# Rows in by sixteen indexed gathers and out by sixteen indexed scatters on GpSimd, in place of eight plain transfers on SyncE

## The chip, the core and the metric

The kernel runs on one core of a Trainium2 chip. The metric is the device time of one execution in microseconds (us). The program is written out by hand: every engine has its own list of instructions, and they meet only at semaphores. The engines are TensorE (PE, its weight loads PEld), VectorE (DVE), ScalarE (ACT), GpSimd (POOL) and SyncE (SP, whose transfer instructions are shown as SPq).

## The reference, cut to what matters

A network of four layers over 8 sequences of 256 tokens with 128 features, 2048 rows of 128 f32 values (512 bytes a row):

```
x = L0_attn_x                      # (8, 256, 128)
... layer norm, mixture-of-experts FFN, 4 linear-attention blocks,
... a second such FFN, a capacity-routed FFN, 16-head causal attention, the routed FFN again
return x                           # (8, 256, 128)
```

Which rows are read and written does not depend on data: row r of the input is token r, and row r of the result is token r. The arithmetic between is the same in both kernels.

## The kernel before

The activations are kept transposed in SBUF, features on the partitions and the 2048 tokens along the free dimension, in four blocks of 512 tokens (`NTB` = 4 blocks of `TB` = 512, `TPB` = 4 tiles of 128 rows to a block, `TILES` = 16 in all).

**Load.** SyncE issues four transfers first of all (L424), each of a block of 512 rows (256 KB) into `x_tok`, with a semaphore `x_loaded[t]` for each block. Behind them stand its loads of the first expert's weights, some twenty small rows of parameters, and the eight large loads of `w0_raw` for the other experts (L443 to L448).

**Constants.** GpSimd meanwhile writes the constants. First comes the identity matrix `ident` (a memset, then an affine select, L2106 and L2108, which announces `ident_ready`), then the mean weights and the epsilons (`const_ready` 1), then selection masks and iotas (`const_ready` 2). Its next work is in the first FFN: one subtraction for each product tile (`fl`, L2138).

**Start of the compute.** TensorE waits for `ident_ready`, then for each block waits for `x_loaded[t]` and transposes its four tiles (L1140). ScalarE copies each block to `xr` (L1530), and TensorE, ScalarE and VectorE do the first layer norm. VectorE begins with `centre` (L2082), made from `ident`, and then splits the first expert's weights (L1550).

**End.** TensorE transposes the four blocks back (L1159), ScalarE copies each to `z` and announces `out_copied` (L1541), and SyncE stores each block with one transfer (L518) and waits for all (`out_stored`). GpSimd has nothing in its list behind the last weight split of the last FFN (L2155).

Of the kernel before, what the change touches and what calls it, by code (L numbers as in the profile page):

```python
# [9 lines left out]
I32 = mybir.dt.int32  # L10
# [4 lines left out]
P = 128  # L15
SEQS, SEQ = 8, 256
TOK = SEQS * SEQ
TB = 512
NTB = TOK // TB
TILES = TOK // P  # L20
TPB = TB // P
# [111 lines left out]
def f32(ap):  # L133
    return ap.bitcast(F32)


def macaron(nc, a, const, out):
# [3 lines left out]
    with es:  # L141
        def sem(name):
            return es.enter_context(nc.semaphore(name))
# [20 lines left out]
        sb = Region(top)  # L164
        xr = sb("xr", [P, TOK])
        z = sb("z", [P, TOK])
# [10 lines left out]
        iota_p = sb("iota_p", [P, 2])  # L177
        iota_t = sb("iota_t", [P, SEQ])
        eps = sb("eps", [P, 3])
        ln_v = sb("ln_v", [P, NTB, TPB])  # L180
        ln_r = sb("ln_r", [P, NTB, TPB])
        ln_t = sb("ln_t", [P, NTB, TPB])
# [29 lines left out]
        x_tok = fd("x_tok", [P, TILES, P])  # L212
# [146 lines left out]
        x_loaded = [sem(f"x_loaded{t}") for t in range(NTB)]  # L359
# [55 lines left out]
        outT_ready, out_copied, out_stored = sem("outT_ready"), sem("out_copied"), sem("out_stored")  # L415
# [3 lines left out]

        @block.sync  # L420
        def _(sp):
            xf = a["L0_attn_x"].rearrange("s t d -> (s t) d")
            for t in range(NTB):
                sp.dma_start(x_tok[:, t * TPB:(t + 1) * TPB, :],  # L424
                             xf[t * TB:(t + 1) * TB, :].rearrange("(q p) d -> p q d", p=P)).then_inc(x_loaded[t], 16)
            sp.dma_start(w0_raw[:, 0, 0:H0], a["L0_ffn_sw1"][0]).then_inc(w0_loaded[0], 16)
            sp.dma_start(w0_raw[:, 0, H0:2 * H0], a["L0_ffn_sw3"][0]).then_inc(w0_loaded[0], 16)
            sp.dma_start(w0_raw[:, 0, 2 * H0:W0].rearrange("p (t d) -> p t d", t=HT0),
# [83 lines left out]
            for e in range(EXP // 2, EXP):  # L512
                load_up(1, e)

            of = out.rearrange("s t d -> (s t) d")
            for t in range(NTB):
                sp.wait_ge(out_copied, t + 1)
                sp.dma_start(of[t * TB:(t + 1) * TB, :].rearrange("(q p) d -> p q d", p=P),  # L518
                             z[:, t * TB:(t + 1) * TB].rearrange("p (q d) -> p q d", q=TPB)).then_inc(out_stored, 16)
            sp.wait_ge(out_stored, 16 * NTB)  # L520

        W0_LOADS, W0_EARLY, W0_LATE = (3, 4, 4), (4, 5, 6, 7), (6, 8, 10, 12)

# [1 line left out]
        def _(pe):  # L525
# [609 lines left out]

            pe.wait_ge(ident_ready, 1)
            for t in range(NTB):
                pe.wait_ge(x_loaded[t], 16)
                for q in range(TPB):
                    ins = pe.transpose(ps[:, XT_BANKS[t], q * P:(q + 1) * P], x_tok[:, t * TPB + q, :], ident[:])  # L1140
                ins.then_inc(xT_ready, 1)
# [961 lines left out]
        def _(pool):  # L2103
            own = Steps(pool, pool_step)

            own.did(pool.memset(ident[:], 0.0))  # L2106
            own.wait()
            pool.affine_select(out=ident[:], in_=ident[:], pattern=[[-1, P]], compare_op=ALU.not_equal,  # L2108
# [35 lines left out]
            def ffn1(call):  # L2144

                def turned(tb):
                    pool.wait_ge(xtf_done, NTB * call + tb + 1)
                    pool.wait_ge(xth_done, NTB * call + tb + 1)
                    w = slice(tb * TPB, (tb + 1) * TPB)
                    pool.tensor_tensor(xt_lo[:, w, :], xtf[:, tb % 2, :].rearrange("p (q d) -> p q d", d=P), f32(xt_hi[:, w, :]),  # L2150
                                       ALU.subtract).then_inc(xt_done, 1)

                def split_low(e):
                    pool.wait_ge(w1_hi_done, call * EXP + e + 1)
                    pool.tensor_tensor(w1_lo[:, e, :], w1_raw[:, e % (EXP // 2), :], f32(w1_hi[:, e, :]), ALU.subtract).then_inc(w1_lo_done, 1)  # L2155

                if call == 1:
                    for e in range(EXP // 2):
                        split_low(e)
                    pool.wait_ge(proj_ready, NTB)  # L2160
                for tb in range(SPB):
                    turned(tb)
                if call == 0:
                    for e in range(EXP // 2):
                        split_low(e)
                for tb in range(SPB, NTB):
                    turned(tb)
                for e in range(EXP // 2, EXP):
                    split_low(e)
# [16 lines left out]
            def attn1():  # L2186

                for s in range(SEQS):
                    for n in range(3):
                        pool.wait_ge(exp_done, 3 * s + n + 1)  # L2190
                        e = ex[:, s % 2, n, :, :].rearrange("p g (h t) -> p g h t", t=P if n == 2 else SEQ)[:, :, :, 0:P]
                        pool.affine_select(out=e, in_=e, pattern=[[0, 4], [0, 4 if n == 2 else 2], [1, P]],  # L2192
                                           compare_op=ALU.is_ge, fill=0.0, base=0, channel_multiplier=-1).then_inc(causal_done, 1)
# [11 lines left out]
            attn1_masks()  # L2205
            attn1()
            ffn1(1)


def _const():  # L2210
# [49 lines left out]
```

## Time and profile before

| | |
|---|---|
| median of 2 runs | 1089.91 us (1087.03 and 1092.79) |
| span of the profiled execution | 1083.3 us |
| between that span and the runs | 3.7 to 9.5 us, 6.6 us to the median |
| busy: PE, DVE, ACT, POOL | 87%, 65%, 57%, 30% of the span |
| on the chain that ended last: PE, DVE, ACT, POOL, DMA | 65%, 18%, 10%, 2%, 0% |

The span runs from the first to the last instruction of the profiled execution. No separate device time of that execution is given, so its own time is read as the median of the runs. The busy shares are averages over the whole span; the chain of waits says for each moment which engine's work the rest waited for. Instructions that issue transfers are not counted as busy.

### The profile page before, as it was taken

Reading aid. Unit: us, or ns where it says so; the run is one execution under the profiler, and the core shown is the slowest. Engines: PE = TensorE matmul, PEld = TensorE weight load, DVE = VectorE, ACT = ScalarE, POOL = GpSimd, SP = SyncE. Lnnn points to the kernel's source line nnn. Section 1 sums busy time; section 2 is a strip of 40 time slices with the busy share of each in tenths; the row PEclk is TensorE's granted clock in tenths of the full one; section 3 lists DMA queues with packets and bytes.
Section 4 is the critical chain, followed back from the end, with each engine's and each line's share of the span. In section 5 each row is a group of like instructions: output and inputs, shape, how many; then the busy total and the mean of one; then the engine's idle time right before and its main releaser. Section 6 shows DMA issues by size and latency. Waiting matters only on the chain.

```text
span 1083.3 us, 13006 instructions
## 1 busy us (share of the span) xinstructions
PE 945.4 (87%) x4507; PEld 638.9 (59%) x4507; DVE 703.1 (65%) x1413; ACT 615.0 (57%) x995; POOL 326.4 (30%) x241
## 2 busy tenths in 40 slices
PE   6899999579999999879999995899777787788997
PEld 4678886223333333337888875688554555465896
DVE  3978887467778777746788887733276556347532
ACT  6455555268888888763555554544644545535443
POOL 1597776000000000002777774200101211313100
PEclk8999999789999999997999998899978879757999
DMA  5225110000000000003321211100000000001001
GB/s 171 42 79 159 65 64 24 0 1 0 1 1 1 0 1 0 1 0 117 81 68 59 68 41 49 49 2 1 1 2 2 4 3 2 4 1 39 2 1 39
DMA packets 30743, 33.64 MB, mean 31 GB/s; under 512 B 2062, under 2 KB 19798, under 8 KB 30678
## 3 DMA queue, kind: packets, MB, share of 16 engines
q1 hardware_dynamic: 30678, 32.81, 10.3%
q8 instruction: 36, 0.59, 0.2%
q14 instruction: 29, 0.24, 0.1%
HBM read 31.36 MB, written 1.18 MB: 30 GB/s over the span
## 4 chain that ended last, share of the span: by engine, by line
PE 65%; DVE 18%; ACT 10%; issue 4%; POOL 2%; DMA 0%; SPq 0%; ACTq 0%; DVEq 0%; POOLq 0%
PE ps L128 10%; PE ps L129 10%; PE ps L130 10%; PE ps L745 5%; PE ps L857 5%; PE ps L878 3%; PE ps L739 2%; PE ps L943 2%; PE ps L723 2%; ACT L1362 2%; ACT ex L1468 2%; DVE smax L2017 2%; POOL fl L2138 2%; PE ps L828 1%; PE ps L731 1%
## 5 line engine op out<-in xcount | busy, mean ns | idle before, releaser
L2138 POOL TENSOR_TENSOR fl<-fp,fh 128x512 fp32r<-128x512 f32 x144 | 223.3, 1566 | 126.8 <-ACT fh L1268 126.6
L1259 ACT ACTIVATE fs<-ps 128x512 f32<-128x512 f32 x144 | 86.4, 600 | 114.5 <-PE ps L130 114.4
L1726 DVE TENSOR_TENSOR fp<-fp,cwb 128x512 f32<-128x512 f32 x128 | 140.8, 1100 | 14.0 <-DVE fp L1719 0.9
L1719 DVE TENSOR_TENSOR fp<-fs,ps 128x512 f32<-128x512 f32 x144 | 98.1, 682 | 40.7 <-ACT fs L1259 40.2
L128 PE MATMUL ps<-z_hi,w_hi 128*128 128x512 f32 x288 | 116.8, 405 | 3.3 <-DVE fp L1719 3.2
L129 PE MATMUL ps<-z_lo,w_hi 128*128 128x512 f32 x288 | 116.0, 403 | 0.0
L130 PE MATMUL ps<-z_hi,w_lo 128*128 128x512 f32 x288 | 115.9, 402 | 0.0
L1268 ACT CAST fh<-fp 128x512 fp32r<-128x512 f32 x144 | 88.8, 617 | 36.8 <-DVE fp L1726 32.7
L2199 POOL TENSOR_TENSOR ln_sq<-ln_rs 128x512 f32<-128x512 f32 x20 | 21.2, 1058 | 272.3 <-ACT ln_rs L1325 272.3
L2192 POOL TENSOR_SCALAR_AFFINE_SELECT ex<-ex 128x1024 f32<-128x1024 f32 (+1 forms) x24 | 33.5, 1406 | 155.2 <-ACT ex L1468 155.2
L2017 DVE TENSOR_REDUCE smax<-ps 128x8 f32<-128x2048 f32 (+1 forms) x24 | 54.9, 2291 | 38.4 <-PE ps L957 33.3
L1409 ACT ACTIVATE hid<-ps 128x512 f32<-128x512 f32 x64 | 38.4, 601 | 50.3 <-PE ps L130 49.5
L128 PEld LDWEIGHTS ps<-z_hi,w_hi 128*128 128x128 f32 x288 | 55.5, 193 | 18.9 <-DVE fp L1719 5.6
L857 PE MATMUL ps<-hid,w 128*128 128x256 f32 x256 | 66.0, 383 | 0.0
L739 PE MATMUL ps<-z,wb 128*128 128x512 f32 x128 | 62.6, 616 | 2.7 <-DVE qq L1823 2.7
L130 PEld LDWEIGHTS ps<-z_hi,w_lo 128*128 128x128 f32 x288 | 55.6, 193 | 12.9
L129 PEld LDWEIGHTS ps<-z_lo,w_hi 128*128 128x128 f32 x288 | 55.4, 192 | 12.6 <-issue 0.2
L128 PE MATMUL ps<-fh,w_hi 128*128 128x512 f32 x144 | 57.5, 399 | 3.8 <-POOL fl L2138 3.8
L731 PE MATMUL ps<-z,wb 128*128 128x512 f32 x96 | 51.1, 675 | 10.7 <-DVE z L1798 10.7
L745 PE MATMUL ps<-hid,wb 128*128 128x512 f32 x128 | 60.1, 593 | 0.0
L727 PE MATMUL ps<-ln_sq,mean_w 128*128 128x512 f32 x72 | 39.3, 628 | 20.1 <-ACT ln_sq L1318 20.1
L129 PE MATMUL ps<-fl,w_hi 128*128 128x512 f32 x144 | 56.8, 395 | 0.0
(264 smaller groups left out, 1997.9 us busy)
## 6 DMA issues: line engine op xcount, KB each, us to landing
cwb<-cw_spread SPq DMA_DIRECT2D x64, 256.0 KB, 3.2
w_raw<-in_L_ffn_w_dram SPq DMA_DIRECT2D x20, 256.0 KB, 2.8
w_raw<-in_L_ffn_w_dram SPq DMA_DIRECT2D x4, 512.0 KB, 5.7
w<-in_L_ffn_w_dram SPq DMA_DIRECT2D x8, 256.0 KB, 4.5
x_tok<-in_L_attn_x_dram SPq DMA_DIRECT2D x4, 256.0 KB, 3.6
wb<-in_L_attn_W_dram SPq DMA_DIRECT2D x1, 1024.0 KB, 6.9
wb<-in_L_attn_W_dram SPq DMA_DIRECT2D x4, 256.0 KB, 4.0
out_dram<-z SPq DMA_DIRECT2D x4, 256.0 KB, 3.0
```

Of the source, the lines that this page charges most:

```text
L128: pe.matmul(out, w_hi, x_hi, start=start, stop=False)
L129: pe.matmul(out, w_hi, x_lo, start=False, stop=False)
L130: return pe.matmul(out, w_lo, x_hi, start=False, stop=stop)
L739: pe.matmul(ps[:, bank, :], wb[:, b, (4 + k) * P:(5 + k) * P], blk(z, t), start=True, stop=True).then_inc(a0_matmul[t], 1)
L745: pe.matmul(ps[:, A0_WO, :], wb[:, b, w], hid[:, k, :], start=(k == 0), stop=(k == FT - 1)).then_inc(a0_matmul[t], 1)
L857: ins = pe.matmul(ps[:, OUT1[n % 2], 0:SEQ], w2[:, e, ft * P:(ft + 1) * P], hid[:, g % RING1, f * SEQ:(f + 1) * SEQ], start=(ft == 0), sto ...
L1259: act.activation(fs[:, n % 2, :], ps[:, n % 2, :], ACT.Silu).then_inc(silu_done, 1)
L1268: act.copy(fh[:, n % RING0, :], fp[:, n % RING0, :]).then_inc(fhi_done, 1)
L1719: dve.tensor_tensor(f, fs[:, n % 2, :], ps[:, 2 + n % 2, :], ALU.mult).then_inc(prod_done, 1)
L1726: dve.tensor_tensor(f, f, cwb[:, x % CW_RING, :], ALU.mult).then_inc(weighed, 1)
L2017: dve.tensor_reduce(smax[:, s % 2, int(k > 0), :, hgs], ps[:, bank:bank + 4, :].rearrange("p g (h t) -> p g h t", h=HG if k == 0 else 2), ...
L2138: pool.tensor_tensor(fl[:, n % RING0, :], fp[:, n % RING0, :], f32(fh[:, n % RING0, :]), ALU.subtract).then_inc(flo_done, 1)
```

## The change

A table `row_id` of 128 x 16 integers is made by GpSimd's iota; its entry (p, t) is 128 t + p. GpSimd then issues sixteen indexed gathers, one for each tile: partition p of the tile receives the input row that `row_id[p, t]` names. Each adds 16 to the semaphore of its block, which therefore is waited for at 64 in place of 16. At the end GpSimd waits for `out_copied` block by block and issues sixteen indexed scatters, one for each tile, and waits for all of them. The four loads and four stores on SyncE and SyncE's waits for them are gone. The same bytes move, in rows of 512 bytes.

```diff
+        row_id = sb("row_id", [P, TILES], I32)
...
-            xf = a["L0_attn_x"].rearrange("s t d -> (s t) d")
-            for t in range(NTB):
-                sp.dma_start(x_tok[:, t * TPB:(t + 1) * TPB, :],
-                             xf[t * TB:(t + 1) * TB, :].rearrange("(q p) d -> p q d", p=P)).then_inc(x_loaded[t], 16)
...
-            of = out.rearrange("s t d -> (s t) d")
-            for t in range(NTB):
-                sp.wait_ge(out_copied, t + 1)
-                sp.dma_start(of[t * TB:(t + 1) * TB, :].rearrange("(q p) d -> p q d", p=P),
-                             z[:, t * TB:(t + 1) * TB].rearrange("p (q d) -> p q d", q=TPB)).then_inc(out_stored, 16)
-            sp.wait_ge(out_stored, 16 * NTB)
...
-                pe.wait_ge(x_loaded[t], 16)
+                pe.wait_ge(x_loaded[t], 16 * TPB)
...
+            xf, of = a["L0_attn_x"].rearrange("s t d -> (s t) d"), out.rearrange("s t d -> (s t) d")
+            own.did(pool.iota(row_id[:], pattern=[[P, TILES]], base=0, channel_multiplier=1))
+            own.wait()
+            for t in range(TILES):
+                pool.indirect_dma_start(x_tok[:, t, :], None, xf, bass.IndirectOffsetOnAxis(row_id[:, t:t + 1], 0)).then_inc(x_loaded[t // TPB], 16)
+
             own.did(pool.memset(ident[:], 0.0))
...
             ffn1(1)
+            for t in range(TILES):
+                if t % TPB == 0:
+                    pool.wait_ge(out_copied, t // TPB + 1)
+                pool.indirect_dma_start(of, bass.IndirectOffsetOnAxis(row_id[:, t:t + 1], 0), z[:, t * P:(t + 1) * P], None).then_inc(out_stored, 16)
+            pool.wait_ge(out_stored, 16 * TILES)
```

The first place is the head of GpSimd's list. Before, it is:

```order
L2248 MEMSET const-uint8-127 128x1
L2102 UNCONDITIONAL_BRANCH [waits barrier_Pool_Activation_PE_DVE_SP_gather]
L2106 MEMSET ident 128x128
L2108 ISA [waits pool_step]
L2108 AFFINE_SELECT ident<-ident 128x128
L2110 MEMSET mean_w 128x128
L2111 MEMSET ones_row 1x128
```

In the changed kernel it is:

```order
L2250 MEMSET const-uint8-127 128x1
L2093 UNCONDITIONAL_BRANCH [waits barrier_Pool_Activation_PE_DVE_SP_gather]
L2098 ISA
L2098 IOTA row_id 128x16
L2101 DMA x_tok<-in_L_attn_x_dram,row_id 128x128 [waits pool_step]
L2101 DMA x_tok<-in_L_attn_x_dram,row_id 128x128 x15
L2103 MEMSET ident 128x128
L2105 AFFINE_SELECT ident<-ident 128x128 [waits pool_step]
```

The iota and all sixteen gathers now stand ahead of the identity matrix and of every other constant.

The second place is the end of GpSimd's list and of SyncE's. Before, SyncE's ends with:

```order
L491 DMA w_raw<-in_L_ffn_w_dram 128x512 [waits w1_lo_done] x4
L518 DMA out_dram<-z 128x4x128 [waits out_copied] x4
L141 UNCONDITIONAL_BRANCH [waits out_stored]
```

In the changed kernel GpSimd's ends with:

```order
L2152 TENSOR_TENSOR w_lo<-w_raw,w_hi 128x512 [waits w1_hi_done] x4
L2208 DMA out_dram<-z,row_id 2048x128 [waits out_copied]
L2208 DMA out_dram<-z,row_id 2048x128 x3
L2208 DMA out_dram<-z,row_id 2048x128 [waits out_copied]
L2208 DMA out_dram<-z,row_id 2048x128 x3
L2208 DMA out_dram<-z,row_id 2048x128 [waits out_copied]
L2208 DMA out_dram<-z,row_id 2048x128 x3
L2208 DMA out_dram<-z,row_id 2048x128 [waits out_copied]
L2208 DMA out_dram<-z,row_id 2048x128 x3
L141 UNCONDITIONAL_BRANCH [waits out_stored]
```

Four scatters follow each of the four waits, on GpSimd, behind its last weight split.

## Rows read from the trace of the kernel before

**Rows 1.** The profile page: the span, and shares of the chain that ended last.
```profile
span 1083.3 us, 13006 instructions
PE 65%; DVE 18%; ACT 10%; issue 4%; POOL 2%; DMA 0%; SPq 0%; ACTq 0%; DVEq 0%; POOLq 0%
```

**Rows 2.** The chain of waits, first 8 us: start us, us, what.
```profile
0.80 0.45 SPq L424
...
1.31 0.49 SPq L424
...
1.84 3.92 DMA x_tok<-in_L_attn_x_dram
...
5.81 1.97 PE ps L1140 x8
```

**Rows 3.** Timeline, GpSimd, first 10 us: start us, us, instruction, [idle before].
```profile
0.37 0.10 POOL L2248 MEMSET const-bfloat16-1.0<- 128x1 bf16 x1
0.41 0.10 POOL L2248 MEMSET const-uint8-127<- 128x1 uint8 x1
0.80 0.20 POOL L2106 MEMSET ident<- 128x128 f32 x1 [0.29 <-POOLq L2248]
1.24 0.29 POOL L2108 TENSOR_SCALAR_AFFINE_SELECT ident<-ident 128x128 f32<-128x128 f32 x1 [0.23 <-POOL ident L2106]
...
5.90 0.13 POOL L2128 IOTA iota_p<- 128x2 f32 x1
6.00 0.34 POOL L2129 IOTA iota_t<- 128x256 f32 x1
```

**Rows 4.** Timeline, TensorE, first 10 us.
```profile
3.76 4.02 PE L1140 MATMUL ps<-ident,x_tok 128*128 128x128 f32 x16 [3.76 <-DMA x_tok<-in_L_attn_x_dram]
```

**Rows 5.** Timeline, SyncE's transfer instructions at the start.
```profile
0.80 2.10 SPq L424 DMA_DIRECT2D x_tok<-in_L_attn_x_dram  x4
...
4.90 0.25 SPq L431 DMA_DIRECT2D prow<-in_L_attn_bk_dram  x1
...
10.11 0.40 SPq L443 DMA_DIRECT2D w_raw<-in_L_ffn_w_dram  x1
...
14.56 2.22 SPq L448 DMA_DIRECT2D w_raw<-in_L_ffn_w_dram  x2
```

**Rows 6.** Waits from 8 to 200 us: engine line waited for, us, times, longest.
```profile
POOL fl L2138 <- ACT fh L1268: 60.1, 29, 24.3
...
DVE par L2090 <- PE ps L1147: 6.2, 1, 6.2
...
DVE w_hi L1550 <- DMA w_raw<-in_L_ffn_sw_dram: 5.6, 1, 5.6
```

**Rows 7.** Groups of GpSimd instructions, by form: busy us, mean ns, idle before.
```profile
L2138 POOL TENSOR_TENSOR fl<-fp,fh 128x512 fp32r<-128x512 f32 x144 | 223.3, 1566 | 126.8 <-ACT fh L1268 126.6
...
L2192 POOL TENSOR_SCALAR_AFFINE_SELECT ex<-ex 128x1024 f32<-128x1024 f32 x16 | 17.6, 1102 | 139.8 <-ACT ex L1468 139.8
...
L2142 POOL TENSOR_TENSOR w_lo<-w_raw,w_hi 128x768 fp32r<-128x768 f32 x4 | 8.6, 2148 | 0.0
```

**Rows 8.** Timeline, GpSimd, its last two rows in the whole span.
```profile
1001.92 3.74 POOL L2155 TENSOR_TENSOR w_lo<-w_raw,w_hi 128x512 fp32r<-128x512 f32 x3
1006.56 1.26 POOL L2155 TENSOR_TENSOR w_lo<-w_raw,w_hi 128x512 fp32r<-128x512 f32 x1 [0.90 <-ACT w_hi L1244]
```

**Rows 9.** Timeline of all engines, from 1064 us to the end.
```profile
1076.53 1.91 PE L1159 MATMUL ps<-ident,xr 128*128 128x128 f32 x16
...
1077.16 2.05 ACT L1541 COPY z<-ps 128x512 f32<-128x512 f32 x4 [2.75 <-PE ps L1159]
1077.78 2.32 SPq L518 DMA_DIRECT2D out_dram<-z  x4
```

**Rows 10.** The four output stores by themselves: duration ns, and time from issue to landing.
```profile
L518 SPq DMA_DIRECT2D out_dram<-z x4: 395/506/736, 1077.8 to 1079.4; - x4
...
DMA to landing us min/median/max: 2.4/3.0/3.5
```

**Rows 11.** The DMA engines from 0 to 30 us: busy tenths in 40 slices; issues, KB each, us to landing.
```profile
DMA  0028999993000006899999999995000000000000
...
w_raw<-in_L_ffn_w_dram SPq DMA_DIRECT2D x4, 512.0 KB, 5.7
x_tok<-in_L_attn_x_dram SPq DMA_DIRECT2D x4, 256.0 KB, 3.6
```

## The prediction, made before the changed kernel was run

> **What bounds the kernel now.** I read the page's shares of the chain first: compute is nearly all of it, and transfers have 0% [rows 1]. Over the whole span, then, the input and the output weigh nothing. But the change touches the two ends only, and at each of them the whole kernel stands in line behind it, so I read the ends by themselves.
>
> At the start the chain is transfer: two issues of the input load on SyncE, then 3.92 us until the second block has landed, then transposes [rows 2]. The reader is to see that the identity matrix, the other thing that the transposes wait for, is long ready: its affine select begins at 1.24 and takes 0.29, so it ends at 1.53 [rows 3], while TensorE starts at 3.76 and is through its sixteen transposes at 7.78, with one pause of about 0.5 us for the second block [rows 2, 4]. At the end ScalarE's first copy starts at 1077.16, SyncE's first store at 1077.78, the last of the four at 1079.4, and the stores land 2.4 to 3.5 us after they are issued [rows 9, 10]; the span ends at 1083.3 [rows 1]. So 5.5 us pass from the first store to the end. GpSimd is idle there, its last instruction ends at 1007.8 [rows 8].
>
> **The unknown: what one indexed transfer occupies GpSimd for.** Call it c. The order shows sixteen of them in a row ahead of `ident` and four behind each wait at the end; GpSimd carries out its list in order, so what follows waits until the transfer's rows have been worked out. The trace before has no transfer on GpSimd, so I bound c. From below: SyncE issues a transfer of a few rows in 0.25 us [rows 5]. From above: GpSimd's heaviest subtraction takes 2.15 us on average [rows 7]. An indexed transfer must read 128 indices and write down 128 sources and 128 destinations, by a program and not by the fixed path that SyncE uses; so it is nearest to a middle-sized instruction of GpSimd's own. Those are the affine selects of 128 x 1024 with 1.10 us and the 128 x 512 subtraction, 1.26 us where nothing disturbs it [rows 7, 8]. I take c = 1.2 us and keep 0.25 and 2.15 as ends.
>
> The Trainium skill, "DMA: Bandwidth & Descriptors", section on latency and other measured facts, gives about 1 us to the first byte of a transfer issued on GpSimd, against some 0.6 us from SyncE, and calls it the cost of the program's writing out. By an estimate with c = 1.0 from that page the sum below would be 27 us instead of 33. No row here shows it.
>
> **The start.**
> - Removed: four loads on SyncE, 2.10 us of its queue [rows 5]. Its later loads move up by that much. Worth nothing: between 8 and 200 us the one wait for a transfer is VectorE's for the first expert's weights, 5.6 us long, and behind it VectorE waits another 6.2 us for TensorE's parameters anyway [rows 6].
> - Added ahead of `ident`: an iota of 128 x 16 with the wait for it. A small instruction and the wait before the next take from 0.80 to 1.24 in the present list [rows 3]; so the first gather begins at about 1.24.
> - Sixteen gathers: 16 x 1.2 = 19.2, to 20.4.
> - The memset and affine select of `ident`: 1.53 - 0.80 = 0.73 [rows 3], so `ident_ready` comes at 21.2 us, where it came at 1.53.
> - The transposes start then, at 21.2 in place of 3.76. They no longer pause between blocks: 4.02 - 0.5 = 3.5 us, done at 24.7. Delay of everything behind: 24.7 - 7.78 = 16.9 us, in general 16c - 2.3.
> - Is the data the later one? The last gather ends its issue at 20.4. A 256 KB block lands 3.6 us after its issue, and the large weight loads, which keep the engines full, take 5.7 [rows 11]. Those are issued from 10.11 to 16.8 now [rows 5], 2.1 us earlier after the change, and are through by about 21. The fourth block is wanted at 21.2 + 2.6 = 23.8, 3.4 us after that last issue. I cost this at nothing, and at 2.3 us at worst (5.7 - 3.4).
> - The other constants come behind `ident` as they do now, in 5 us [rows 3], beside transposes and layer norm. GpSimd's next work begins at 30.68 now, after 24.3 us of idleness [rows 6], and moves with the rest. VectorE's splitting of the first weights starts later too, behind `centre`, but it has the 6.2 us of slack named above.
> - Is the delay caught up later? Only if a stage waited for something that now arrives relatively earlier, a transfer. There is none [rows 6]. The delay stays whole.
>
> **The middle.** GpSimd's list is unchanged there, and the transfers there are SyncE's. Nothing.
>
> **The end.**
> - Removed: SyncE's four stores, 5.5 us from first issue to the end.
> - Added: the wait for block 1 passes at the same point. Scatters take 4.8 us a block at c = 1.2, the copies come 0.5 us apart (four in 2.05) [rows 9], so only the first wait counts: 16 x 1.2 = 19.2 us of issue. Then the last one has to land: 3.0 us from issue to landing less its 0.5 us of issue, 2.5 us [rows 10], and the 0.2 us that the end of the program takes. Sum 21.9, against 5.5: 16.4 us more, in general 16c - 2.8.
>
> **Sum:** 16.9 + 16.4 = 33.3 us (32c - 5.1). The profiled execution's span would be 1083.3 + 33.3 = 1116.6. Around the span lie 6.6 us to the median of the two runs, 1089.91, which are 5.8 us apart, and I take that to stay: **1123 us**. The ends of c give 32 x 0.25 - 5.1 = +2.9 (1093) and 32 x 2.15 - 5.1 = +63.7 (1154), 1156 with the late landing.
>
> A measurement of this kernel can tell about 2% from no change, 21.8 us. That is passed where c is above (21.8 + 5.1) / 32 = 0.84 us.
>
> **The rivals.**
> 1. *Cheap issue, not slower* (0.17). GpSimd hands the indexed transfer on as quickly as SyncE does its own, 0.25 to 0.5 us, and the sixteen issues flow. For it: they are small, 64 KB each, and GpSimd's smallest instructions follow one another within 0.04 us [rows 3]. Against it: there are 128 indices to be read and no fixed path. Its place is the run of sixteen at either end, its price 32c - 5.1; with c = 0.4, +7.7 us, 1098 us. It decides below c = 0.84.
> 2. *Index by index* (0.05). Each index costs a step of its own that does not overlap the next. The smallest step of GpSimd in the trace is the 0.04 us between two memsets of one column [rows 3]; 128 of them are 5.1 us a transfer, and 32 x 5.1 - 5.1 = +158 us, 1248 us. Against it: an iota that writes all 128 partitions is done in 0.13 us [rows 3], so the partitions are not gone through one by one there. The Trainium skill, "GPSIMD Engine Reference", section on performance pitfalls, warns of about 102 cycles for each small read command, as in one per gather index, that do not overlap. By an estimate from that page (at 1.2 GHz) a transfer would take 10.9 us and the kernel some 1430 us; no row here bears on it.
> 3. *Half of it* (0.05). The start is absorbed: the gathers delay only the constants, and the first stages catch up because GpSimd or VectorE had slack in them. Then only the end is left, +16.4 us, 1106 us. Against it is the absence of waits for transfers.
> 4. *The change does not do what it says* (0.02): the eight loads' time was on the path, and the many small transfers arrive earlier block by block, so that it gains. The most there is to gain is the wait before 3.76 us and the 0.5 us pause, about 2 us: 1088 us.
>
> **How the numbers follow.** My forecast, c from 0.84 to 2.15, has 0.71. The range is to hold 8 in 10. I cut a little of the upper end and take in part of the cheap rival: c = 0.55 gives +12.5, 1102 us; c = 1.9 gives +55.7 and with 2.3 for late landing +58, 1148 us. Outside are the rest of rival 1, rivals 2 and 4 and a twentieth at the upper end. Slower by over 2%: 0.71 + 0.05, with a little of the third rival where c is above 1.2, 0.77. Within 2%: 0.21. Faster: 0.02, since even free issues only gain about 5 us, 0.5%.
>
> **What would show it.** The interval from one gather to the next on GpSimd is c. The first transpose should start at about 21 us, waiting for `ident` and not for `x_tok`; `ident_ready` just before it; the first `fl` of GpSimd near 47.6 instead of 30.68. At the end the first scatter should follow the first copy by 0.6 us, and the last come 18 us after it, with nothing on any other engine. The middle, from first transpose of the start to the first copy of the end, should keep its length: from 3.76 to 1077.16 now, 0.5 us less then. The prediction is wrong if c is below 0.84, if the middle changes its length, or if the transposes wait for the gathers' landing.

## The result, and the profile after

The changed kernel takes 1120.47 us (median of 2 runs, 1118.23 and 1122.72), before 1089.91: ratio 1.032, 95% interval 1.026 to 1.038. Timed once more in e1 (4 runs against 7) it is 1.035, interval 1.029 to 1.040. It is slower, and by what was forecast (1123 us, range 1102 to 1148).

The page of the changed kernel shows the span and the chain's shares, to be held against [rows 1]:

```profile
span 1116.5 us, 13031 instructions
PE 63%; DVE 17%; ACT 10%; POOL 5%; issue 4%; DVEq 0%; ACTq 0%; POOLq 0%
```

GpSimd's share of the chain rose from 2 to 5%. The profiled execution took 1118.23 us, 1.7 more than its span.

GpSimd's timeline at the start, where [rows 3] had `ident` at 0.80 (start us, us, instruction, idle before):

```profile
0.92 0.14 POOL L2098 IOTA row_id<- 128x16 int32 x1 [0.40 <-POOLq L2250]
1.71 1.12 POOL L2101 DMA_INDIRECT x_tok<-in_L_attn_x_dram,row_id  x1 [0.65 <-POOL row_id L2098]
3.14 0.96 POOL L2101 DMA_INDIRECT x_tok<-in_L_attn_x_dram,row_id  x1 [0.31 <-issue]
...
19.39 0.94 POOL L2101 DMA_INDIRECT x_tok<-in_L_attn_x_dram,row_id  x1 [0.30 <-issue]
20.64 0.94 POOL L2101 DMA_INDIRECT x_tok<-in_L_attn_x_dram,row_id  x1 [0.30 <-issue]
21.58 0.22 POOL L2103 MEMSET ident<- 128x128 f32 x1
21.96 0.29 POOL L2105 TENSOR_SCALAR_AFFINE_SELECT ident<-ident 128x128 f32<-128x128 f32 x1 [0.16 <-POOL ident L2103]
```

Each gather is busy for 0.94 us and another 0.30 passes before the next, though GpSimd waits for nothing: c is the interval, 1.25 us. The row of TensorE that answers to [rows 4] waits for `ident` and no longer for `x_tok`:

```profile
22.31 3.52 PE L1131 MATMUL ps<-ident,x_tok 128*128 128x128 f32 x16 [22.31 <-POOL ident L2105]
```

At the end, in place of [rows 9], the timeline of all engines shows the copies and the first and last two of sixteen scatters:

```profile
1091.28 2.05 ACT L1532 COPY z<-ps 128x512 f32<-128x512 f32 x4 [2.75 <-PE ps L1150]
1092.15 1.04 POOL L2208 DMA_INDIRECT out_dram<-z,row_id  x1 [69.53 <-ACT z L1532]
1093.50 0.97 POOL L2208 DMA_INDIRECT out_dram<-z,row_id  x1 [0.30 <-issue]
...
1109.92 0.96 POOL L2208 DMA_INDIRECT out_dram<-z,row_id  x1 [0.31 <-issue]
1111.18 0.96 POOL L2208 DMA_INDIRECT out_dram<-z,row_id  x1 [0.30 <-issue]
```

Once ScalarE's copies are done no other engine computes anything. Asked for the scatters alone (landing) and for the line that ends the program (each instruction's duration in ns and its start), the trace of the changed kernel gives:

```profile
DMA to landing us min/median/max: 2.2/2.2/2.3
```
```profile
L141 POOLq COMPARE_BRANCH  x1: 38/38/38, 1113.4 to 1113.4; - x1
L141 POOLq DRAIN  x1: 2681/2681/2681, 1113.6 to 1113.6; - x1
L141 SPq EVENT_SEMAPHORE  x1: 17/17/17, 1116.4 to 1116.4; - x1
```

The last scatter lands at 1111.2 + 2.2 = 1113.4 and GpSimd's wait is over then. Every engine's list ends with an instruction called a drain, and only after GpSimd's, of 2.68 us, can the engines meet. That drain was not in the forecast. In the kernel before it lay at 1006.5, long covered, and ended with GpSimd's last subtraction (1.26 us from 1006.56, [rows 8]), so that its 1.37 us are that instruction's and not its own:

```profile
L141 POOLq DRAIN  x1: 1372/1372/1372, 1006.5 to 1006.5; - x1
```

So the kernel divides into three parts, and this division carries the rest: the start up to the end of the transposes, the middle up to ScalarE's first output copy, and the end.

| us | start | middle | end | span |
|---|---|---|---|---|
| before | 7.8 | 1069.4 | 6.1 | 1083.3 |
| changed | 25.8 | 1065.5 | 25.2 | 1116.5 |
| difference | +18.1 | -3.9 | +19.1 | +33.2 |

### The profile page after: what moved, and what is told of

Its sections match the earlier page's. It is cut to its first block, busy times and chain, and to the rows that moved or that the text cites. A ratio compares the mean times of both kernels' runs of the same rounds, so it can differ in the third digit from the quotient of the medians.

```text
span 1116.5 us, 13031 instructions
## 1 busy us (share of the span) xinstructions
PE 942.4 (84%) x4507; PEld 638.5 (57%) x4507; DVE 704.1 (63%) x1413; ACT 615.3 (55%) x995; POOL 358.7 (32%) x274
## 4 chain that ended last, share of the span: by engine, by line
PE 63%; DVE 17%; ACT 10%; POOL 5%; issue 4%; DVEq 0%; ACTq 0%; POOLq 0%
PE ps L128 10%; PE ps L129 10%; PE ps L130 10%; PE ps L736 5%; PE ps L848 5%; PE ps L869 3%; PE ps L730 2%; PE ps L934 2%; PE ps L714 2%; ACT L1353 2%; PE ps L819 2%; ACT ex L1459 2%; POOL fl L2135 2%; POOL out_dram L2208 1%; PE ps L722 1%
## 5 line engine op out<-in xcount | busy, mean ns | idle before, releaser
L1717 DVE TENSOR_TENSOR fp<-fp,cwb 128x512 f32<-128x512 f32 x128 | 141.0, 1102 | 14.0 <-DVE fp L1710 0.9
L1710 DVE TENSOR_TENSOR fp<-fs,ps 128x512 f32<-128x512 f32 x144 | 98.2, 683 | 36.9 <-ACT fs L1250 35.6
```

The source lines that it names most:

```text
L1710: dve.tensor_tensor(f, fs[:, n % 2, :], ps[:, 2 + n % 2, :], ALU.mult).then_inc(prod_done, 1)
L1717: dve.tensor_tensor(f, f, cwb[:, x % CW_RING, :], ALU.mult).then_inc(weighed, 1)
```

## The experiments

**e1, the changed kernel again.** No edit.

> The changed kernel once more, to see which parts of its trace repeat. Theory (the two ends carry the whole difference, each sixteen transfers of 1.25 us on GpSimd): first transpose at 22.3 us, end of the transposes at 25.8; from ScalarE's first output copy to the end of the span 25.2 us; both within 0.1 us of the first trace. The part between, 1069.4 us before and 1065.5 in the first trace of the changed kernel, should scatter by several us, since nothing in it was changed; the time is 1.03 of before. Rival (the change really shortens the middle, by what it leaves to SyncE or by a later start): the middle is again about 1065.5, at most 1066.5.

Measured: start 26.0, middle 1066.7, end 25.2, span 1117.9; the profiled execution took 1119.64 us, the four runs 1118.21 to 1123.73. The ends repeat (the start is 0.2 us longer because TensorE's sixteen transposes took 3.68 us). The middle came out near the first one. At 1066.7 it misses the rival's bound of 1066.5 by 0.2 us, so this trace alone does not decide. But the other runs of this same kernel have spans from 1116.5 to 1122.0 us, and with the ends fixed only the middle can hold that: 5 us of scatter. The kernel before scatters more. It was executed 48 times beside the experiments, with spans from 1077.2 to 1090.4 us (23 of them together, beside e10 and e11, from 1077.9 to 1090.4); less the 13.9 us of its two ends that is a middle from 1063.3 to 1076.5, half of them above 1069.9. The six executions of the changed kernel (two at first, four here) have 1065.3 to 1070.8 by the same reckoning, inside that spread. Over all fourteen traces of this study the middle lies between 1065.5 and 1073.9, though no compute instruction in it was changed (of the strided transposes of e6 and e10 to e12 only those of the first output block fall into it).

**e2, gathers only.**

```diff
+            for t in range(NTB):
+                sp.wait_ge(out_copied, t + 1)
+                sp.dma_start(of[t * TB:(t + 1) * TB, :].rearrange("(q p) d -> p q d", p=P),
+                             z[:, t * TB:(t + 1) * TB].rearrange("p (q d) -> p q d", q=TPB)).then_inc(out_stored, 16)
+            sp.wait_ge(out_stored, 16 * NTB)
...
-                pool.indirect_dma_start(of, bass.IndirectOffsetOnAxis(row_id[:, t:t + 1], 0), z[:, t * P:(t + 1) * P], None).then_inc(out_stored, 16)
-            pool.wait_ge(out_stored, 16 * TILES)
```

> Gathers on GpSimd at the start, the output by SyncE's four stores. Theory: transposes end at 25.8 us, 18.1 later than before, the end takes 6.1 us as before; 1090 + 18 = 1108 us, ratio 1.017. The extra tail of about 2.5 us between the last landing and the end of the span is gone if it belongs to GpSimd's waiting for its own last transfers; if it belongs to having used GpSimd's transfer queue at all, the end takes 8.5 us. Rival (the start is absorbed by slack later): ratio 1.00 to 1.005.

Measured: start 26.0, middle 1067.4, end 6.1; 1101.57 us, ratio 1.017 (1.012 to 1.022). It is slower than before; whether by 2%, this interval leaves open. The start's delay arrives at the end and the absorbed rival is out. The drain costs nothing: it stands at 1022.7, while the others still work. Of its 3.43 us the first 2.1 are a wait for GpSimd's last subtraction, whose row of four (L2158, 5.00 us from 1019.76) ends at 1024.8; the 1.4 us behind it are the drain's own, some 1000 us after the gathers landed.

```profile
L141 POOLq DRAIN  x1: 3428/3428/3428, 1022.7 to 1022.7; - x1
```

**e3, scatters only.**

```diff
+            for t in range(NTB):
+                sp.dma_start(x_tok[:, t * TPB:(t + 1) * TPB, :],
+                             xf[t * TB:(t + 1) * TB, :].rearrange("(q p) d -> p q d", p=P)).then_inc(x_loaded[t], 16)
...
-                pe.wait_ge(x_loaded[t], 16 * TPB)
+                pe.wait_ge(x_loaded[t], 16)
...
-                pool.indirect_dma_start(x_tok[:, t, :], None, xf, bass.IndirectOffsetOnAxis(row_id[:, t:t + 1], 0)).then_inc(x_loaded[t // TPB], 16)
```

> SyncE's four loads at the start, the output by sixteen scatters. Theory: transposes end at 7.8 us as before (7.9 with the iota ahead of the identity matrix, hidden by the load), from the first copy to the end 25.2 us, 19.1 more than before; 1109 us, ratio 1.0175; with e2 the two add up to the whole change, 37 us less what the middle scatters. Rival (the ends interact): their sum differs from the whole by over 5 us.

Measured: start 8.0, middle 1069.6, end 24.1; 1101.87 us, ratio 1.016 (1.010 to 1.021), again slower with 2% left open. The two halves add up: 1.68% + 1.56% = 3.2%, the whole 3.5% (2.9 to 4.0). The end is 1.1 us shorter than the expected 25.2, and the drain says why: after sixteen transfers it takes half of what it took after thirty-two.

```profile
L141 POOLq DRAIN  x1: 1374/1374/1374, 1100.1 to 1100.1; - x1
```

**e4, the identity matrix ahead of the gathers.**

```diff
+            own.did(pool.memset(ident[:], 0.0))
+            own.wait()
+            pool.affine_select(out=ident[:], in_=ident[:], pattern=[[-1, P]], compare_op=ALU.not_equal,
+                               fill=1.0, base=0, channel_multiplier=1).then_inc(ident_ready, 1)
             own.did(pool.iota(row_id[:], pattern=[[P, TILES]], base=0, channel_multiplier=1))
...
-            own.did(pool.memset(ident[:], 0.0))
-            own.wait()
-            pool.affine_select(out=ident[:], in_=ident[:], pattern=[[-1, P]], compare_op=ALU.not_equal,
-                               fill=1.0, base=0, channel_multiplier=1).then_inc(ident_ready, 1)
```

> The identity matrix is made ahead of the gathers, all else as in the changed kernel. Theory (GpSimd's sixteen issues are the floor, whatever stands before or behind them): the transposes of block 1 begin when its four gathers have landed, near 9 to 11 us, but the last block's only when the sixteenth gather, issued by 22.3, has landed, 2.4 us later or more: near 25 us, and its four transposes end at 25.5 to 26.5, so no gain against 25.8; ratio 1.03. Rival (the late identity matrix is the cost, the order in GpSimd's list): the transposes are over at once when the gathers end, near 23 us, ratio 1.027.

Measured: TensorE's transposes start early and then wait for the gathers (timeline, TensorE):

```profile
8.57 1.09 PE L1131 MATMUL ps<-ident,x_tok 128*128 128x128 f32 x4 [8.57 <-DMA x_tok<-in_L_attn_x_dram,row_id]
17.81 1.11 PE L1131 MATMUL ps<-ident,x_tok 128*128 128x128 f32 x4 [8.15 <-DMA x_tok<-in_L_attn_x_dram,row_id]
22.25 2.29 PE L1131 MATMUL ps<-ident,x_tok 128*128 128x128 f32 x8 [3.32 <-DMA x_tok<-in_L_attn_x_dram,row_id]
```

They end at 24.5, between the two expectations: 1.5 us earlier than in e1, because the last block had landed by 23.4, 2.4 us after its issue at 21.03. The theory's "no gain" is missed by that much. The time is the same, 1122.79 us, ratio 1.035 (1.029 to 1.040). So the late `ident` is mostly the form the wait took; behind it stood the gathers themselves. GpSimd's sixteen issues and the last landing are the floor.

The same trace shows that a gather can land late. The gathers by themselves:

```profile
DMA to landing us min/median/max: 2.4/4.3/6.7
```

The last gather of block 2 is issued at 11.04 and TensorE waits for it until 17.81, while SyncE's large weight loads are under way. The last block escapes this, since the traffic of those loads ends near 22 us.

**e5, thirty-two gathers of 64 rows.** Output by SyncE. The lines are shown against the changed kernel; with them `row_id` becomes 64 x 32 and a block is waited for at 32 x 4 = 128.

The kernels of e5 to e9 were executed once each. Their times carry the scatter of the middle, so they are judged by rows and by the two ends.

```diff
-                pool.indirect_dma_start(x_tok[:, t, :], None, xf, bass.IndirectOffsetOnAxis(row_id[:, t:t + 1], 0)).then_inc(x_loaded[t // TPB], 16)
+                for h in range(2):
+                    pool.indirect_dma_start(x_tok[h * 64:(h + 1) * 64, t, :], None, xf,
+                                            bass.IndirectOffsetOnAxis(row_id[:, 2 * t + h:2 * t + h + 1], 0)).then_inc(x_loaded[t // TPB], 16)
```

> Thirty-two gathers of 64 rows each in place of sixteen of 128, output by SyncE's four stores. The interval between gathers was 1.25 us with 128 rows. Theory A (a fixed cost for each transfer): the interval stays at 1.15 to 1.25 us, the first transpose starts at 2.1 + 32 x 1.2 = 40 to 42 us. Theory B (a cost for each row): 0.62 to 0.7 us, first transpose near 22 us. Between: the two intervals give both terms.

Measured (timeline, GpSimd; two of the thirty-two):

```profile
4.31 0.90 POOL L2108 DMA_INDIRECT x_tok<-in_L_attn_x_dram,row_id  x1 [0.30 <-issue]
5.52 0.90 POOL L2108 DMA_INDIRECT x_tok<-in_L_attn_x_dram,row_id  x1 [0.30 <-issue]
```

The interval is 1.21 us against 1.25: half the rows save 0.04 us, 0.6 ns a row, and 1.17 us are fixed. The first transpose starts at 41.0 us and the start takes 44.7, 36.9 more than before: as much as the whole change (1122.59 us). Theory A holds.

**e6, rows of 2 KB: four gathers, four scatters.** A row is now four tokens, all on one partition. The scatters and the output transposes change in the same way.

```diff
+            xf, of = a["L0_attn_x"].rearrange("s (t q) d -> (s t) (q d)", q=TPB), out.rearrange("s (t q) d -> (s t) (q d)", q=TPB)
+            for t in range(NTB):
+                pool.indirect_dma_start(x_tok[:, t * TPB:(t + 1) * TPB, :].rearrange("p q d -> p (q d)"), None, xf,
+                                        bass.IndirectOffsetOnAxis(row_id[:, t:t + 1], 0)).then_inc(x_loaded[t], 16)
...
-                    ins = pe.transpose(ps[:, XT_BANKS[t], q * P:(q + 1) * P], x_tok[:, t * TPB + q, :], ident[:])
+                    ins = pe.transpose(ps[:, XT_BANKS[t], :].rearrange("c (p q) -> c p q", q=TPB)[:, :, q], x_tok[:, t * TPB + q, :], ident[:])
```

> The same bytes with a quarter of the indices: a row is four tokens of one partition (2 KB), so four gathers and four scatters of 128 rows; TensorE's transposes read or write every fourth column to undo it. If the cost is for each transfer or for each index, the interval stays at 1.25 us: first transpose near 1.7 + 4 x 1.25 + 0.7 = 7.4 us, transposes end near 11 us, and from first copy to the end 5 + 2.5 + 3 = 10.5 us: 1090 + 3.2 + 4.4 = 1098 us. If the cost is for each 512 bytes: the interval is near 4 us and the time as the changed kernel's, 1120 us.

Measured: the interval is 1.25 to 1.27 us with four times the bytes (timeline, GpSimd, the second to the fourth gather):

```profile
3.15 0.96 POOL L2102 DMA_INDIRECT x_tok<-in_L_attn_x_dram,row_id  x1 [0.31 <-issue]
4.42 0.95 POOL L2102 DMA_INDIRECT x_tok<-in_L_attn_x_dram,row_id  x1 [0.31 <-issue]
5.67 0.95 POOL L2102 DMA_INDIRECT x_tok<-in_L_attn_x_dram,row_id  x1 [0.30 <-issue]
```

The start takes 11.0 us, the end 8.5; 1095.26 us beside 1084.81 of the kernel before, each executed once. The ends explain 3.2 + 2.4 = 5.6 us of these 10.5, the rest is mostly the middle of that execution, 1073.9, which lies within the spread of the kernel before. The forecast for the ends was 7.6; the end is shorter because the drain after eight transfers takes only 0.72 us (the program's last line, by itself):

```profile
L141 POOLq DRAIN  x1: 721/721/721, 1092.6 to 1092.6; - x1
```

**e7 and e8, GpSimd's transfers without indices**, sixteen and sixteen of 128 rows (e7), four and four of 512 rows (e8). Shown are e7's loads; its stores and e8's transfers follow the same pattern, and `row_id` is still made.

```diff
-                pool.indirect_dma_start(x_tok[:, t, :], None, xf, bass.IndirectOffsetOnAxis(row_id[:, t:t + 1], 0)).then_inc(x_loaded[t // TPB], 16)
+                pool.dma_start(x_tok[:, t, :], xf[t * P:(t + 1) * P, :]).then_inc(x_loaded[t // TPB], 16)
```

> Sixteen loads and sixteen stores on GpSimd without indices, each of the same 128 rows of 512 bytes. Theory (working out 128 sources and destinations by a program is the cost, the index only an added read): the interval is 0.9 to 1.2 us and the time 1108 to 1120 us. Rival (the indices are the cost): 0.3 to 0.5 us, the time 1092 to 1098 us.

> Four loads and four stores on GpSimd without indices, 512 rows each. If a transfer costs a fixed time: interval 1 to 1.3 us, time 1095 to 1098 us. If every row costs: 2.5 to 4 us, so that the four together take as long as the sixteen, 1108 to 1120 us.

Measured, GpSimd's timeline of e7 and of e8 (each row merges all the loads):

```profile
1.46 8.73 POOL L2101 DMA_DIRECT2D x_tok<-in_L_attn_x_dram  x16 [0.41 <-POOL row_id L2098]
```
```profile
1.46 3.13 POOL L2101 DMA_DIRECT2D x_tok<-in_L_attn_x_dram  x4 [0.40 <-POOL row_id L2098]
```

A plain transfer of 128 rows takes 8.73 / 16 = 0.55 us and one of 512 rows 3.13 / 4 = 0.78: again 0.6 ns a row, on a fixed 0.47. So of the 1.25 us of a gather 0.55 are there without any index and 0.70 come with the indexed form, 0.30 of them as the gap between two. Neither expectation of e7 had it: the time, 1103.99, lies between the two. In e7 the start is 17.3 and the end 13.8, in e8 9.9 and 8.1 (1090.23 us). e8's time is 5 us below its expectation: the interval is 0.78 and not 1 to 1.3.

e7's start is not the issue alone. Its last load is issued at 9.6 and `ident` is ready at 10.85, but the last block lands only at 16.2, and TensorE waits for it:

```profile
16.19 1.11 PE L1131 MATMUL ps<-ident,x_tok 128*128 128x128 f32 x4 [2.46 <-DMA x_tok<-in_L_attn_x_dram]
```

That landing took 6.5 us, beside SyncE's weight loads, as in e4.

**e9, SyncE waits for the last stores.**

```diff
-            pool.wait_ge(out_stored, 16 * TILES)
+            sp.wait_ge(out_stored, 16 * TILES)
```

(the second line in SyncE's list)

> The changed kernel, except that SyncE waits for the last stores and GpSimd's list ends with its last scatter. In the traces so far GpSimd ends the program with a drain that begins when its wait for the stores is over and takes 2.68 us after thirty-two transfers. Theory (the drain is work on the transfers issued, and can lie beside the last landing): it begins right behind the last issue, about 1.2 us earlier, and the span ends 23.7 to 24.1 us after ScalarE's first output copy, in place of 25.2. Rival (the drain waits for the landing itself, so that the wait was never what delayed it): 25.2 us as before.

Measured: the end takes 1116.3 - 1092.57 = 23.7 us, 1.5 less than in e1. The line that ends the program shows GpSimd's drain waiting in its queue from 1098.3 on and over at 1116.1, 2.7 us after its last scatter's issue (1112.47 + 0.96):

```profile
1112.47 0.96 POOL L2209 DMA_INDIRECT out_dram<-z,row_id  x1 [0.31 <-issue]
```
```profile
L141 POOLq DRAIN  x1: 17817/17817/17817, 1098.3 to 1098.3; - x1
L141 SPq COMPARE_BRANCH  x1: 33/33/33, 1114.7 to 1114.7; - x1
```

The landing is over at 1114.7, so the drain and not the data ends the program. Had its 2.7 us begun with the landing, as in e1, it would have ended near 1117.4. It does not need the landing.

**e10 to e12, rows of 2 KB on SyncE's plain transfers**: does e6's layout help the kernel before? e10 has it at both ends, e11 too, with blocks 2 and 4 issued by ScalarE, e12 at the output only. Shown are the output's lines, which all three share; the loads of e10 and e11 change in the same way, and the transposes are strided as in e6.

```diff
-            of = out.rearrange("s t d -> (s t) d")
+            of = out.rearrange("s (t q) d -> (s t) (q d)", q=TPB)
             for t in range(NTB):
                 sp.wait_ge(out_copied, t + 1)
-                sp.dma_start(of[t * TB:(t + 1) * TB, :].rearrange("(q p) d -> p q d", p=P),
-                             z[:, t * TB:(t + 1) * TB].rearrange("p (q d) -> p q d", q=TPB)).then_inc(out_stored, 16)
+                sp.dma_start(of[t * P:(t + 1) * P, :], z[:, t * TB:(t + 1) * TB]).then_inc(out_stored, 16)
```

> The kernel before with SyncE's plain transfers, but rows of 2 KB (four tokens of one partition) in place of 512 bytes; TensorE's transposes read or write every fourth column. In the trace before, 1 MB of output in 512-byte rows takes 5.5 us from first issue to the end, paced at 260 to 340 GB/s; in e6 the same bytes in 2 KB rows moved at up to 400 GB/s. Theory: the last store lands 0.5 to 1 us earlier and the second input block 0.2 to 0.5 us earlier; together 0.7 to 1.5 us, 0.1%, below what five rounds tell (ratio 0.996 to 1.002), so it is read from the two ends in the trace: transposes end at 7.3 to 7.6 us (7.78 before), the end takes 5.2 to 5.6 us (6.1 before).

> As e10, and the input blocks 2 and 4 are issued by ScalarE at its very start, beside SyncE's 1 and 3. Theory: block 2 is issued at 0.8 in place of 1.3 us, so TensorE's pause for it goes; transposes end at 6.9 to 7.3 us. ScalarE's own load of its table of functions moves by 1 us and is hidden, since its first copy comes at 4.9. Ratio 0.995 to 1.002. Rival (the four blocks share the same sixteen transfer engines, so an earlier issue of block 2 delays block 1): the first transpose starts later than 3.76 and the end of the transposes stays at 7.5 or more.

> The kernel before with its own input loads (512-byte rows) and only the stores in 2 KB rows. In e10 and e11 the end, from ScalarE's first output copy to the end of the span, took 5.1 us against 6.1, and the transposes of the start ended at 8.3 us against 7.8. Theory: the start stays at 7.8, the end takes 5.1 us: 1.0 us less than before, 0.1%, which five rounds cannot tell (ratio 0.996 to 1.002). Rival (the end's gain came from the faster start or from chance): 6.1 us.

Measured: the end takes 5.1 us in all three (6.1 before), and the stores land sooner than in [rows 10] (the stores of e12 by themselves):

```profile
L518 SPq DMA_DIRECT2D out_dram<-z x4: 338/342/351, 1079.5 to 1081.0; - x4
DMA to landing us min/median/max: 2.0/2.3/2.6
```

The start does not gain, against the expectations of e10 and e11: transposes end at 8.3 there, and at 8.1 in e12 with the loads unchanged (8.0 in e3), so 0.3 us of this is scatter. In e11 TensorE starts at 4.6 instead of 3.8 and then runs without a pause, as its rival said. Its blocks land 3.7 to 4.7 us after issue, in e10 2.7 to 4.8; that they share the same transfer engines is the rival's reading and fits. Ratios with five rounds: 0.998 (0.995 to 1.001), 0.997 (0.995 to 1.000), 1.000 (0.998 to 1.002). The 1.0 us of the end is in the traces; none of the three is shown to be faster than the kernel before.

## Why the prediction was right, and where by luck

- **Bound at the two ends only.** Right. e2 and e3 have the delays separately, and they add.
- **c.** Taken as 1.2, measured 1.25 for gathers and 1.26 for scatters. The forecast took it from GpSimd instructions of middle size and argued by the work on 128 indices. The number was near, the reason was not: e5 shows 1.17 us of it fixed. That 64 rows cost nearly as much as 128 was not foreseen, nor that a 2 KB row costs no more than one of 512 bytes (e6).
- **The start.** Forecast: transposes over at 24.7; measured 25.8. Of the 1.1 us, 0.5 is the first gather, which starts at 1.71 and not at 1.24, the rest the interval. Late landing was costed at nothing and was nothing, because the last block is issued late enough; e4 and e7 show landings of 6.5 to 6.7 us, and a shorter run of issues meets them (e7). `ident` was named as what the transposes wait for, and it was; but e4 shows that it hid a second wait, nearly as long. One reading of the kernel before was off by a block: the pause of TensorE before 5.81 stands behind eight transposes and in front of eight [rows 2], so it is for block 3 and not for block 2, here and in e11's expectation. The sum does not depend on it.
- **The slack.** That nothing takes up the delay held (e2: end unchanged, start +18).
- **The end.** Forecast 22.5 us from first copy to the end (0.6 to the first store and 21.9), measured 25.2. Here a step failed: "the 0.2 us that the end of the program takes". It takes 3.1 us, from 1113.4 to 1116.5, and 2.68 of them are GpSimd's drain. Against it stood a landing over 1.3 us after the last issue and not 2.5, the figure taken from the 256 KB stores of [rows 10]; the scatters' longer issue and the later first one (0.87 us behind the first copy) make up another 1.1.
- **The middle.** Forecast unchanged, measured 3.9 us shorter, which is one of the signs that the prediction itself named for being wrong. The 48 executions of the kernel before (e1) take that sign away: their middles lie 13 us apart. That scatter goes with TensorE's mean granted clock over the span, which is listed for each execution. The 15 of the 48 with 0.924 or more have spans of 1077.2 to 1082.1 us, the 19 with 0.917 or less have 1083.1 to 1090.4. What makes the clock differ stays open. Between the two kernels the clock does not explain the shorter middle: over the span it is 0.920 before and 0.910 after, but over the middle 0.92 in both, and much of the difference comes from the end, where TensorE stands idle through the scatters (0.62 over these 25.2 us, 0.98 over the 6.1 before). The four traces with sixteen gathers ahead of `ident` (the changed kernel, e1, e2, e9) have the lowest middles, 1065.5 to 1067.4, the ten others 1069 or more; but the other executions of the changed kernel, e1 and e2 reach 1071, so I take it for scatter. A part of an effect, of 1 or 2 us, is not excluded.
- **Around the span.** The 6.6 us were a misreading: with the profiled execution's own time known, a span lacks 1.7 us of its run. The execution profiled before was a quicker one than either of the two runs shown.

Errors of +1.1 (start), +2.7 (end) and -3.9 (middle) cancel; the span came out at 1116.5 against 1116.6 forecast. The mechanism was right, the closeness is chance. By the ends alone the change costs 18.1 + 19.1 = 37.1 us, 3.4%, inside e1's interval of 2.9 to 4.0%.

The rivals: cheap issue (c below 0.84) and index by index (5 us and more) are refuted by the interval of 1.25 us, the absorbed start by e2, and a gain at either end by e2 and e3, each slower by itself. The page "DMA: Bandwidth & Descriptors" of the Trainium skill, with its 1 us to the first byte, would have given 27 us by the prediction's estimate; the trace shows no first byte but an engine held for 1.25 us. The same page of the Trainium skill, in its section on the anatomy of a transfer on this path, gives a fit of 2.0 us plus bytes over 436 GB/s. For 64 KB that is 2.15 us by estimate. The scatters' landing, 2.2 us, agrees; e7's plain stores of the same size land in 1.8, and the gathers beside the weight loads take up to 6.7.

## What to carry to other kernels

Count the transfers that GpSimd issues, not their rows or bytes: an indexed one holds it for about 1.2 us whether it has 64 or 128 rows and whether a row has 512 bytes or 2 KB, so use all partitions and make the rows long (measured for 64 and 128 rows, 512 bytes and 2 KB). Put them where GpSimd is idle and nobody waits: here both ends were places where the whole kernel stands behind them, and in e2 GpSimd's drain, covered by the other engines' work, was free. Where the order is known beforehand, a plain transfer by SyncE costs neither.

## What the runs showed of the hardware that was not expected

- GpSimd's last instruction of the program, a drain, grows with the number of transfers issued there: 0.72 us after 8 (e6), 1.37 after 16 (e3), 2.68 after 32 (changed kernel, e1, e4, e7), that is 0.08 us a transfer, indexed or plain. In e2, after 16, its own part is 1.4 us as well, long after the gathers landed. Where GpSimd has issued no transfer its own part is under 0.1 us: in the kernel before it ends with the last subtraction. After transfers it begins behind the last issue and runs beside the landing if another engine waits for the stores (e9).
- The cost a row is 0.6 ns in both kinds of transfer: 128 against 64 rows indexed, 512 against 128 plain.
- Two gathers or scatters in a row are 0.30 us apart with nothing waited for; plain transfers of GpSimd follow one another without a gap (e7).
- The kernel before takes 1077.9 to 1090.4 us from first to last instruction over 23 executions made together, and the longer ones have the lower mean granted clock. Traces of single executions cannot compare middles to better than that.
